# Moving the row transposes, the value products and the projection within a unit of a fused attention and expert kernel

## What is computed

```python
xn = _layernorm(x)                          # x: 16 batches, 512 rows, 256 columns, fp32
# attention: 16 heads of 64
q, k, v = split(xn @ wqkv.T)
q = rope(rmsnorm(q, q_norm_w)); k = rope(rmsnorm(k, k_norm_w))
attn = softmax(where(causal, q @ k.T * 64 ** -0.5, -inf))
a = (attn @ v) @ wo.T
# experts: each row goes through one of 8 matrices of 256 x 256
chosen = argmax(xn @ gate_w.T)
f = xn + expert_w[chosen] @ xn
return x + a + f
```

## Time and profile before

| What | Value |
|---|---|
| time, median of 3 runs | 2036.11 us (2035.03 to 2037.41) |
| the profiled execution: its own time | 2035.76 us |
| its span, from the first to the last instruction | 2033.9 us |
| PE busy | 1966.9 us, 97% |
| DVE busy | 1741.2 us, 86% |
| ACT busy | 1607.6 us, 79% |
| POOL busy | 1377.0 us, 68% |
| mean granted TensorE clock | 0.992 |

### The profile page before, as it was taken

One profiled execution on the slowest core, in us unless ns is written; L12 is line 12 of the kernel. 1 busy time (PEld: TensorE's weight loads), 2 busy tenths in 40 slices (PEclk: granted clock), 3 DMA queues, 4 the chain that ended last, 5 costly groups with the idle time before them and its releaser, 6 DMA issues.

```text
span 2033.9 us, 48319 instructions
## 1 busy us (share of the span) xinstructions
PE 1966.9 (97%) x16520; PEld 1642.1 (81%) x16520; DVE 1741.2 (86%) x4144; ACT 1607.6 (79%) x5095; POOL 1377.0 (68%) x1975
## 2 busy tenths in 40 slices
PE   4899999999999999999999999999999999999997
PEld 4777888888888888888888888888888888888885
DVE  5799888888888888888988889889888888888875
ACT  3787788888788788787878878878888887888775
POOL 6567766577666767658766686666876677766764
PEclk8999999999999999999999999999999999999999
DMA  5111211112211132111221122221222112222244
GB/s 188 58 48 40 68 48 61 61 45 77 92 61 48 46 102 79 54 58 59 73 94 48 48 79 73 74 63 53 64 74 84 48 53 84 69 68 64 82 133 148
DMA packets 84548, 145.81 MB, mean 72 GB/s; under 512 B 9808, under 2 KB 63184, under 8 KB 84176
## 3 DMA queue, kind: packets, MB, share of 16 engines
q1 hardware_dynamic: 78160, 125.93, 19.3%
q0 software_dynamic: 6144, 16.79, 2.5%
HBM read 102.05 MB, written 40.63 MB: 70 GB/s over the span
## 4 chain that ended last, share of the span: by engine, by line
PE 82%; POOL 6%; DVE 5%; ACT 4%; issue 2%; DMA 0%; POOLq 0%; DVEq 0%
PE ps_g L737 36%; PE ps_g L834 14%; PE ps_s L823 11%; PE ps_g L843 11%; PE ps_g L799 5%; PE ps_s L816 3%; POOL rms_inv L526 2%; POOL qk_rot L520 2%; ACT prob L618 2%; POOL qk_rot L531 2%; PE ps_g L764 1%; DVE qk_sin L1013 1%; DVE qk_cos L1013 1%; PE ps_g L746 1%; ACT qk_sq L602 1%
## 5 line engine op out<-in xcount | busy, mean ns | idle before, releaser
L520 POOL TENSOR_TENSOR qk_rot<-qk_cos,qk_sin 128x128 f32<-128x128 f32 x1024 | 466.6, 477 | 577.6 <-DVE qk_sin L1013 572.3
L737 PE MATMUL ps_g<-w_qkv,xn_t 128*128 128x384 f32 (+1 forms) x3072 | 640.2, 351 | 2.3 <-DVE xn_t L928 1.5
L618 ACT ACTIVATE prob<-ps_s,neg_max 128x256 f32<-128x256 f32 (+3 forms) x1024 | 536.3, 550 | 0.3 <-DVE neg_max L1027 0.3
L737 PEld LDWEIGHTS ps_g<-w_qkv,xn_t 128*128 128x128 f32 x3072 | 526.6, 190 | 5.5 <-issue 2.2
L526 POOL TENSOR_TENSOR rms_inv<-ss,neg_half 128x8 f32<-128x8 f32 x256 | 448.6, 1752 | 0.0
L1027 DVE TENSOR_REDUCE neg_max<-ps_s 128x2 f32<-128x512 f32 (+3 forms) x512 | 404.8, 810 | 0.0
L628 ACT ACTIVATE prob_t<-ps_g 128x512 f32<-128x512 f32 (+2 forms) x768 | 370.1, 526 | 37.5 <-PE ps_g L834 37.5
L834 PE MATMUL ps_g<-ident,prob 128*128 128x128 f32 x2560 | 361.7, 278 | 3.9 <-DVE prob L1038 1.6
L834 PEld LDWEIGHTS ps_g<-ident,prob 128*128 128x128 f32 x2560 | 290.3, 141 | 74.3 <-DVE prob L1038 45.1
L531 POOL TENSOR_TENSOR qk_rot<-qk_rot,rms_inv 128x256 f32<-128x256 f32 x512 | 324.1, 654 | 20.1
L843 PE MATMUL ps_g<-prob_t,v 128*64 128x512 f32 (+3 forms) x2048 | 305.6, 441 | 1.0 <-ACT prob_t L628 1.0
(11 more groups left out here) (108 smaller groups left out, 2517.8 us busy)
## 6 DMA issues: line engine op xcount, KB each, us to landing
w_tile<-w_dram SPq DMA_DIRECT2D x120, 512.0 KB, 3.5
x_rows_s<-x_dram SPq DMA_DIRECT2D x120, 128.0 KB, 2.1
y_dram<-y_rows_s SPq DMA_DIRECT2D x120, 128.0 KB, 1.7
xin<-in_x SPq DMA_DIRECT2D x16, 512.0 KB, 4.2
out<-acc SPq DMA_DIRECT2D x15, 512.0 KB, 3.3
w_dram<-w_tile SPq DMA_DIRECT2D x8, 512.0 KB, 3.0
x_dram<-xn SPq DMA_DIRECT2D x2, 1920.0 KB, 18.0
y_back<-in_expert_t SPq DMA_DIRECT2D x8, 256.0 KB, 3.7
```

The lines of the kernel that those rows point to most:

```text
L520: r = pool.tensor_tensor(rot[:, :, a, :], cos[:, :, a, :], sin[:, :, 1 - a, :], ALU.add)
L618: r = act.activation(prob[:, h, prob_at(k):prob_at(k) + w], ps_s[n % 2][:, h, 0:w], ACT.Exp, bias=neg_max[:, i, h:h + 1], scale=1.0, accum ...
L737: r = pe.matmul(ps, lhs(a, c), rhs(b, c), start=(c == parts[0] and (a, b) == TERMS[0]), stop=(c == parts[-1] and (a, b) == TERMS[-1]))
```

## The change

The change moves steps within a turn on TensorE and on ScalarE, and the list `uses` with them. No instruction is added or taken away, and VectorE, GpSimd and SyncE keep their order.

- The transposes of the first two sorted tiles come right behind the first visit, ahead of the transposes of probabilities.
- Behind qkv3 come the first expert product and the transpose of a third tile, or the projection where a turn has no tile; then the values, then the second visit.
- ScalarE takes the sorted rows first in a turn, and the values behind the first expert result.

```diff
@@ uses(u)
+            found += [f"xs{i}" for i in tiles[0:2]]
             if live(u - 1):
                 found += ["pt2.0", "pt2.1", "pt3.0"]
-            found += [f"xs{i}" for i in tiles[0:2]]
             if live(u + 1):
                 found += ["qkv3"]
+            found += [f"ex{i}" for i in tiles[0:1]] + [f"xs{i}" for i in tiles[2:3]]
+            if projection(u) and not tiles:
+                found += ["proj"]
             if live(u - 1):
                 found += ["o"]
-            found += [f"ex{i}" for i in tiles[0:1]] + [f"xs{i}" for i in tiles[2:3]]
...
-            if projection(u):
+            if projection(u) and tiles:
                 found += ["proj"]
@@ ScalarE, unit(u)
+                for i in tiles[0:2]:
+                    take_xs(u, i)
                 if live(u - 1):
                     take_pt(u - 1, 2)
                     take_pt(u - 1, 3)
-                for i in tiles[0:2]:
-                    take_xs(u, i)
...
-                if live(u - 1):
-                    take_o(u - 1)
...
                 for i in tiles[2:3]:
                     take_xs(u, i)
+                if live(u - 1):
+                    take_o(u - 1)
@@ TensorE, unit(u)
                 if live(u):
                     scores(u, 0)
+                for i in tiles[0:2]:
+                    transpose_xs(u, i)
                 if live(u - 1):
                     transpose_probs(u - 1, 2)
                     transpose_probs(u - 1, 3)
-                for i in tiles[0:2]:
-                    transpose_xs(u, i)
                 if live(u + 1):
                     qkv(u + 1, 3)
-                if live(u - 1):
-                    values(u - 1)
                 for i in tiles[0:1]:
                     expert(u, i)
                 for i in tiles[2:3]:
                     transpose_xs(u, i)
+                if projection(u) and not tiles:
+                    project(u)
+                if live(u - 1):
+                    values(u - 1)
                 if live(u):
                     scores(u, 2)
...
-                if projection(u):
+                if projection(u) and tiles:
                     project(u)
```

## The result

| | median | span | mean granted clock | TensorE busy | turn with one tile |
|---|---|---|---|---|---|
| before, timed again beside it | 2035.57 us | 2033.9 us | 0.992 | 97% | 15.15 us |
| after | 2208.36 us (2207.62 to 2211.96) | 2206.8 us | 0.991 | 90% | 16.62 us |

The changed kernel takes 1.0851 times the time of the one before (95% interval 1.0837 to 1.0864). It is slower by 172.8 us, where 171.4 were forecast.

A forecast was written before the change was run, and what follows sets the result against it. TensorE, busy 97%, was taken to bound the kernel, with the changed loop going round over VectorE. 180.4 (wait) - 13 (joint) + 3 (turns without a tile) + 1 (end) = +171.4 us on 2036.1, 2207 us; range 2170 to 2250.

The forecast's parts named there:

- new wait: TensorE at qkv3, held until VectorE ends the sorted rows' rest (L985): 1.67 us later, 108 times, 180.4 us.
- chain of 9.61: From the start of L799 over TensorE, ScalarE and VectorE to the end of L985: 9.61 us without slack.
- chain of 7.15: TensorE's work from qkv3's load to the next L799: 7.15 us of the turn.
- saved joint: Between qkv3 and the second visit, one idle joint of weight loads fewer: 0.15 us less a turn, 13 us in all.
- later pt2.0: Transposes of probabilities start 0.42 us later for their bank: no cost under cover, up to 0.2 us a turn without.
- Turns without a tile: Sixteen turns with the projection put ahead of the values: +3 us in total, range -5 to +12.
- The end: Turn 128's last values come behind a projection and the last two projections need them: +1 us, range 0 to 1.4.
- The clock falls: Rival: TensorE's idle time of about 1.5 us a turn brings half clock in half the turns, +92, 2299 us; chance 0.10.
- Half absorbed: Rival: slack between L799 and L985 lets only half of 1.67 us through, 2117 us; chance 0.08.
- Faster: Rival: the sorted rows' bank is free when TensorE reaches qkv3, leaving only the saved joint, 2020 us; chance 0.04.
- No change: Rival: bank free at qkv3, but the later pt2.0 eats the saved joint, +0.05 us a turn, 2041 us; chance 0.04.
- What would show it: Signs in the profile after: qkv3 waiting for VectorE's rest about 108 times, some 160 us; tile turn 16.7 us; TensorE near 89%.

The follow-up runs named there:

- rows_only: Kernel before with only the sorted rows' transposes and copies moved ahead of the probabilities on TensorE and ScalarE; 2216.73 us, 1.0879.
- rest_first: Changed kernel with VectorE's rest of the sorted rows put ahead of both row maxima of the first visit; 2055.05 us, 1.0094.
- expert_only: Kernel before with only the expert product moved ahead of the values on TensorE and ScalarE; 2074.59 us, 1.0182.
- proj_undone: Changed kernel without the move of the projection in turns without a tile; 2201.14 us, 1.0800.
- proj_only: Kernel before with only the projection moved ahead of the values in the sixteen turns without a tile; 2048.88 us, 1.0052.
- bank_skip: Changed kernel with one bank of the rotation skipped ahead of qkv3 in turns with a tile; 2098.19 us, 1.0292.
- max_double: Changed kernel with the first visit's second row maximum computed twice in turns with a tile, ahead of the sorted rows' rest; 2445.64 us, 1.2005.
- amid: Kernel before with sorted rows between the two transposes of probabilities, VectorE's rest between the row maxima, expert product ahead of values; 2035.48 us, 0.9983.
- rows_back: Changed kernel with sorted rows transposed and copied behind the probabilities again, the rest of the change kept; 2083.03 us, 1.0225.
- rest_between: Changed kernel with VectorE's rest of the sorted rows between the first visit's two row maxima; 2086.85 us, 1.0247.

## Why the prediction held, and where its terms were off

**The bound and the new wait: right, and shown.** Rows_only gave 1.65 us for each of 108 turns, its one stretch of half clock left out, where the prediction had 1.67, and rest_first took the wait away by moving L989 alone. The chain of 9.61 and the chain of 7.15 less 0.15 us were measured as 9.66 and 6.95.

**Where the second move stood.** The prediction costed the expert product ahead of the values as a gain only. That holds behind the new wait. On its own the move costs 0.42 us a turn (expert_only), because it needs the same VectorE result. The prediction's statement that nobody near needs that result was true for the order of before alone; the sum was not touched, as one wait covers the other, but the rivals were.

**The saved joint: right in kind, a little more.** Between rows_only and proj_undone, which differ by that move, lie 1778.5 - 1762.2 = 16.3 us in the 104 turns and 0.9 in the last four. Less the 1.6 us of half clock in rows_only's turn 122 that makes 15.6 us, where I had taken 13. In plain turns it is 0.20 us (16.82 to 16.62).

**The later pt2.0: right that it costs nothing here.** Its price showed once the cover was gone: rest_first has the saved joint but a turn of 15.17 us, against 15.15 before. The transposes of probabilities sit idle for 0.30 us behind the rows' transposes, marked "issue"; I had put the price at up to 0.2 us a turn. Whether VectorE's products or TensorE itself holds them there, no run here shows.

**Turns without a tile: mis-sized.** I took +3 with a range up to +12; measured were +8.0 in turns 3 to 12 and +4.5 in the six single ones, 12.5 us. For the single ones the mechanism was right (qkv0 waits until the projection is added) and so was its upper bound, 0.76 against 0.75 measured; the step that failed was that I let it go to +0.5. For turns 3 to 12, which I had put near 0, a term was missing. I had followed the projection's bank to qkv0 and not looked at which use stands four places later in turn 6, where two transposes of rows lie between. That turn went from 15.57 to 17.35 us in proj_only. In the kernel after it took 18.95, and turn 8 took 17.73 where it took 16.17 at full clock in bank_skip: each holds a stretch of half clock, 1.6 us. So of the 8.0 us, some 3.2 are the clock and 1.8 the wait in turn 6. Another 2.6 are turns 4, 7, 8 and 12, 0.64 to 0.68 us each with the clock left out: there qkv0 waits for the added projection as in the single turns, 0.50 us by the matmuls in proj_only.

**The end:** I took +1 for it; the part behind the last first visit is 0.2 us shorter. With 32.7 to 36.4 us over the kernels it can't be resolved, and I leave it open.

**The sum.** In the traces: 155.2 (the 104 turns with a tile) + 5.6 (turns 123 to 126) + 12.5 (without a tile) - 0.4 (start and end) = 172.9 us, the difference of the spans. Forecast for the first two were 180.4 - 13 = 167.4, and 160.8 came. The forecast was 6.6 us too high there and 9.5 too low in the turns without a tile, so that part of its closeness is luck: two errors against each other. Of the 6.6 us, 2.6 are the joint and 2.5 the wait (177.9 for 180.4, the half clock of turn 122 left out). The last 1.5 lie between proj_undone and the kernel after; half of them are the seven turns right behind the turns without a tile, 16.52 us where proj_undone has 16.63.

**The rivals.** *The clock falls:* not in the turns with a tile of this kernel; 1.47 us of idle loads in a turn (1.23 by the matmuls) left it at 1.00, though rows_only, with the same wait, had one stretch at 0.50 in its 108 turns. In one turn of the kernel after, with the columns of the earlier trace rows:

```profile
1140.20:1143.60 3.40, 2.09 (x17) 1.27 (x13) 3.32 (x7) 2.42 (x6) 3.32 (x5) 1.00 0.00 0
1143.60:1147.00 3.40, 3.40 (x20) 2.43 (x22) 1.09 (x3) 2.06 (x9) 0.76 (x3) 1.00 0.03 5
```

With 2.49 us by the matmuls it fell (max_double), and then by nearly what the rival had: 64 of 108 turns at 1.6 us, for its 54 at 1.7. *Half absorbed:* turns with extra work on VectorE grew much like the plain ones, whose growth is 1.47: 16.04 to 17.52, 15.80 to 17.48, the least 15.34 to 16.57. The mean over the 104 turns is 1.49, so hardly anything was absorbed. *Faster:* its condition is met in rest_first, and the kernel was still not faster; the rival had left out the later pt2.0 and the projection. Even amid gives 0.17%, not the 0.8% that I put on it. *No change:* ruled out by the wait. Where the wait is gone, in rest_first, the later pt2.0 does eat the saved joint as the rival said, 15.17 us against 15.15.

**What would show it.** 103 waits of 1.45 us, 149 us by the loads (108 and 160 said; in turns 122 to 126, which have two or three tiles, it is L836 that waits for L989, 1.32 us each by the matmuls); a turn of 16.62 us (16.7); VectorE idle 2.00 us before the rope products in the turn shown (nearly 2); TensorE busy at 90% (89); clock 0.991 (0.99). The entry at the first visit's end did not move to VectorE's rope product: it is marked "issue" now.

**The rule of the Trainium skill** (TensorEngine Tiling (Array Packing), Key Properties), that a change of tiling mode drains TensorE: the runs agree with it and size it. One change fewer in a turn gave 0.20 us in plain turns.

## What to carry to other kernels

In a rotation of banks, moving one step changes who waits for whom four uses away: list each use's predecessor in the new order, in the odd turns too, and look up when that one's last reader is done. Then compare that time with when the bounding engine gets there, and follow the chain back to the bounding engine itself; if it closes without slack, the loop's time is the length of the chain, and one turn's rows give it to some hundredths. When a moved step needs an engine's result sooner, move that engine's instruction as well, and expect the next wait to be close behind.

## What I had not expected of the hardware

- The granted clock answered abruptly to a longer wait. With TensorE's matmuls idle for 1.23 us in each turn of 16.6 us (the loads for 1.47) the granted clock stayed at 1.00 in the turns with a tile of the kernel after; with 2.49 us (2.70) in turns of 17.9 us it went down to its lower level in 64 of 108 such turns, at 1.6 us each. In turn 6 an idle time of 2.26 us was followed by such a stretch in the kernel after (18.95 us) and by none in proj_only (17.35 us), whose turn does the same work; there the stretch came in turn 8 (0.50 from 178.2 to 181.6 us). Why the one and not the other is open.
- An idle time that a trace puts down to another engine can be TensorE's own. The 0.36 us of idle loads behind the first visit is marked as a wait for VectorE's scaling in the kernel before and in rows_back, and as "issue", of the same length, in the kernel after, where the sorted rows stand there. The 0.17 us before the second visit is marked as "issue" in rows_back and as a wait for the exponentials in amid.
- In the rows shown a weight load that truly waited started 0.05 to 0.06 us behind the end of its cause: 1143.52 to 1143.58 in the kernel after, 1052.20 to 1052.25 in rest_between.
